# New column group bounds, an earlier residual add, an earlier mean and split last rows in a windowed-attention and feed-forward kernel on eight cores

## What is computed

```python
q = (x @ Wq + bq)  # 16 heads of 64
k = (x @ Wk + bk)  # 2 key heads
v = (x @ Wv + bv)
# each position attends to the 256 positions from 128 before to 127 after it
probs = softmax(scores);  out = probs @ v_win
x = layernorm(x + out @ Wo + bo)
# feed-forward part, x_prev is x shifted by one position
xr = mu_r * x + (1 - mu_r) * x_prev
xk = mu_k * x + (1 - mu_k) * x_prev
x = layernorm(x + sigmoid(xr @ W_r) * (square(relu(xk @ W_k)) @ W_v))
```

## Time and profile before

| | us |
|---|---|
| three runs, median (lowest to highest) | 502.43 (499.56 to 543.57) |
| the profiled execution | 499.95 |
| its span on the slowest core, core 6 | 498.4 |
| spans of the eight cores | 490.4 to 498.4 |
| PE (matmul) busy on core 6 | 424.5, 85% of the span |
| ACT, DVE, POOL busy | 331.9, 316.1, 115.7 |

### The profile page before, as it was taken

The page is one execution under the profiler, slowest core; times in us unless marked ns, Lnnn a source line. Parts: engine busy times, 40 slices in busy tenths (PEclk is TensorE's granted clock), DMA queues, the critical chain, the costliest instruction groups (busy, mean ns, idle before and its releaser), DMA issues.

```text
span 498.4 us, 10425 instructions; the slowest of 8 cores (490.4 to 498.4 us)
## 1 busy us (share of the span) xinstructions
PE 424.5 (85%) x2976; PEld 221.0 (44%) x3018; DVE 316.1 (63%) x792; ACT 331.9 (67%) x847; POOL 115.7 (23%) x297
## 2 busy tenths in 40 slices
PE   0878999689989888699799889998979989999990
PEld 0344444344444445464355345454335345464640
DVE  0046775355565667847887797997796897536321
ACT  1276879548585947685669579859669769455632
POOL 4222124022141214010123032132114033130303
PEclk9996999979989995989999999999999999999995
DMA  7999937948473758332157759766956849512112
GB/s 103 163 167 210 149 45 124 181 77 160 74 117 65 142 94 153 59 85 45 42 52 150 172 103 169 172 109 156 160 125 139 164 91 171 122 42 64 43 44 85
DMA packets 73864, 57.16 MB, mean 115 GB/s; under 512 B 59344, under 2 KB 60496, under 8 KB 73808
## 3 DMA queue, kind: packets, MB, share of 16 engines
q0 software_dynamic: 11600, 24.88, 31.9%
q1 hardware_dynamic: 62208, 31.61, 28.7%
HBM read 49.76 MB, written 8.39 MB: 117 GB/s over the span
## 4 chain that ended last, share of the span: by engine, by line
PE 55%; ACT 15%; issue 9%; DVE 9%; DMA 7%; POOL 2%; ACTq 0%; DVEq 0%; POOLq 0%; SPq 0%
PE pm L300 11%; PE pm L288 9%; PE pm L318 7%; PE pm L328 7%; PE po L353 6%; PE pm L310 5%; ACT p L392 5%; PE psc L243 4%; DVE nmax L537 4%; PE pm L267 3%; DMA zx<-xres 3%; DMA bufq<-wq 3%; ACT junk L473 2%; DVE zb L587 1%; ACT junk L490 1%
## 5 line engine op out<-in xcount | busy, mean ns | idle before, releaser
L392 ACT ACTIVATE p<-psc,nmax 128x320 bf16<-128x320 f32 x264 | 138.4, 538 | 93.8 <-DVE nmax L537 93.6
L537 DVE TENSOR_REDUCE nmax<-psc 128x2 f32<-128x640 f32 x132 | 108.0, 820 | 84.4 <-PE psc L249 84.0
L300 PE MATMUL pm<-w16o,ao 128*128 128x512 bf16 x262 | 65.9, 393 | 9.5 <-DVE zx L573 5.3
L549 DVE TENSOR_SCALAR p<-p,rall 128x320 bf16<-128x320 bf16 x264 | 62.6, 300 | 7.5 <-DVE rall L542 0.5
L288 PE MATMUL pm<-bufx,bufq 128*128 128x512 bf16 (+2 forms) x310 | 64.3, 353 | 2.6 <-issue 1.4
L310 PE MATMUL pm<-bufx,w16kf 128*128 128x256 bf16 x512 | 62.0, 277 | 2.7 <-ACT pt L406 1.6
L318 PE MATMUL pm<-w16r,bufx 128*128 128x512 bf16 x246 | 57.5, 379 | 3.9 <-ACT pt L406 1.6
L328 PE MATMUL pm<-w16vf,bufq 128*128 128x512 bf16 x247 | 58.1, 379 | 2.9 <-ACT pt L406 2.0
L392 ACT ACTIVATION_READ_ACCUMULATOR p<-psc,nmax 128x1 f32 x264 | 56.5, 214 | 0.0
L310 PEld LDWEIGHTS pm<-bufx,w16kf 128*128 128x128 bf16 x512 | 49.1, 99 | 14.1 <-issue 6.5
L243 PE MATMUL psc<-k,qy 64*128 64x320 bf16 x264 | 41.8, 314 | 11.9 <-ACT p L392 11.6
(11 more groups left out here) (75 smaller groups left out, 545.1 us busy)
## 6 DMA issues: line engine op xcount, KB each, us to landing
zx<-bo SPq DMA_DIRECT2D x17, 512.0 KB, 5.5
zx<-xres POOLq DMA_DIRECT2D x17, 512.0 KB, 6.0
out<-zb SPq DMA_DIRECT2D x16, 512.0 KB, 3.0
bufx<-xt POOLq DMA_DIRECT2D x16, 256.0 KB, 8.4
bufq<-wq POOLq DMA_DIRECT2D x4, 512.0 KB, 10.3
w16o<-wo POOLq DMA_DIRECT2D x8, 256.0 KB, 12.5
w16kf<-wkf POOLq DMA_DIRECT2D x8, 256.0 KB, 5.7
w16r<-wr POOLq DMA_DIRECT2D x8, 256.0 KB, 5.9
```

Source lines behind the costliest of these rows:

```text
L300: mm = e.matmul(pm[:, bank, :], ao[:, a % 2, kc, :], w16o[:, kc, 512 * b:512 * b + 512], start=(kc == 0), stop=(kc == KC - 1))
L392: a = e.activation(p16[:, b % 2, j // 2, g, j % 2, :], psc[:, 2 * (n % 2) + g, 0:320], AF.Exp, bias=nmax[:, n % 4, g:g + 1], accum_out=sal ...
L537: e.tensor_reduce(nmax[:, n % 4, :], psc[:, 2 * (n % 2):2 * (n % 2) + 2, 0:320], mybir.AxisListType.X, ALU.max, negate=True).then_inc(s_mx, 1)
L549: t = e.tensor_scalar(part, part, rall[:, b % 2, r:r + 1], None, ALU.mult)
```

## The change

The groups become 384, 512, 512, 512 and 448 columns wide, with explicit starts `XO`. The units of group 1 start in slot 4 and those of group 2 in slot 22; groups 3 and 4 keep their slots. `add_xres` comes four slots after `rows_y`, not six. `layer_norm` on POOL is split in two: `mean`, which waits only for the row sums, and `scale`, which waits for the squares; together they have one small instruction less. For the last 128 rows, the second sum, the squares, the final scaling and the store are done in halves of 512 columns; the second half of the final scaling goes to DVE. The core of the diff (the last rows on ACT, and the changed indexing on the host, are left out):

```diff
-XW = (512, 512, 512, 512, 320)
+XW = (384, 512, 512, 512, 448)
+XO = (0, 384, 896, 1408, 1920)
 QLO = (128, 0, 0, 0, 0)
-QHI = (512, 512, 512, 512, 192)
-GSLOT = (None, 8, 24, 36, 48)
+QHI = (384, 512, 512, 512, 320)
+GSLOT = (None, 4, 22, 36, 48)
...
-            if b % 8 == 6 or b == 0:
-                e.wait_ge(s_ea, ACT_COUNT[INDEX[("q", (b + 2) // 8, 2 * j + 1)]])
+            if b == 0 or 64 * b + 128 in XO:
+                e.wait_ge(s_ea, ACT_COUNT[INDEX[("q", group(64 * b + 128), 2 * j + 1)]])
...
+        def second_sum_half(half):
+
+            r = 2 * NH - 1
+            e.wait_ge(s_ed, DVE_COUNT[INDEX[("v", r, half)]])
+            if half == 0:
+                e.wait_ge(s_ln2, r - 1)
+            z = zb[:, r % 2, 512 * half:512 * half + 512]
+            e.scalar_tensor_tensor(z, z, 0.5, qy[:, r + 1, 4 * half:4 * half + 4, :].rearrange("p a b -> p (a b)"),
+                                   ALU.mult, ALU.add,
+                                   accum_out=st2[:, r % 2, half:half + 1]).then_inc(s_z2, 1)
...
+        r = 2 * NH - 1
+        e.wait_ge(s_ln2, r + 1)
+        e.tensor_scalar(zb[:, r % 2, 512:1024], zb[:, r % 2, 512:1024], st2[:, r % 2, 8:9], st2[:, r % 2, 9:10],
+                        ALU.mult, ALU.add).then_inc(s_oh, 1)
...
-            small(e.tensor_tensor(stat[:, 5:6], stat[:, 4:5], stat[:, 4:5], ALU.mult))
-            small(e.tensor_scalar(stat[:, 6:7], stat[:, 2:3], 1.0 / D, 1e-5, ALU.mult, ALU.add))
-            small(e.tensor_tensor(stat[:, 7:8], stat[:, 6:7], stat[:, 5:6], ALU.subtract))
+            small(e.tensor_scalar(stat[:, 5:6], stat[:, 4:5], stat[:, 4:5], 1e-5, ALU.mult, ALU.subtract))
+
+        def scale(stat, two, masked, done):
+
+            total = stat[:, 2:3]
+            if two:
+                small(e.tensor_tensor(stat[:, 6:7], stat[:, 2:3], stat[:, 11:12], ALU.add))
+                total = stat[:, 6:7]
+            small(e.tensor_scalar(stat[:, 7:8], total, 1.0 / D, stat[:, 5:6], ALU.mult, ALU.subtract))
...
+                e.wait_ge(s_ed, DVE_COUNT[INDEX[("o", tau, 1)]])
+                mean(st1[:, tau % 2, :], True)
                 e.wait_ge(s_sq1, tau + 1)
-                layer_norm(st1[:, tau % 2, :], True, tau == 0, s_ln1)
-            if n - 6 in YOUT[:NT - 2]:
-                add_xres(YOUT.index(n - 6) + 2)
+                scale(st1[:, tau % 2, :], False, tau == 0, s_ln1)
+            if n - 4 in YOUT[:NT - 2]:
+                add_xres(YOUT.index(n - 4) + 2)
```

More of the change, by code:

```diff
@@ L49, in plan_units @@
         us = [("K", g, 0), ("V", g, 0), ("W", g, 0), ("W", g, 1)] + [("q", g, dc) for dc in range(8)]
-        todo.update({n: [u] for n, u in zip(free, us)})
+        for n, u in zip(free, us):
+            todo.setdefault(n, []).append(u)
     ffn = [("k", j) for j in range(4)] + [(a, t, nh) for a in "rv" for t in range(2) for nh in range(2)]
@@ L225, in build_nc, with group @@
     s_p, s_ln1, s_ln2 = sem("s_p"), sem("s_ln1"), sem("s_ln2")
+    def group(column):
+        return max(g for g in range(5) if XO[g] <= column)
     def key_group(b):
-        return min((64 * b + 319) // 512, 4)
+        return group(64 * b + 319)
     def value_group(b):
-        return min((b // 2 + 2 + b % 2) // 4, 4)
+        return group(min(128 * (b // 2 + 2 + b % 2), XC - 1))
     def tensor(e):
@@ L411, in evac @@
                 if kind == "K":
-                    dst = k16[:, 512 * a:512 * a + XW[a]]
+                    dst = k16[:, XO[a]:XO[a] + XW[a]]
                 else:
-                    dst = vt[:, 64 + 512 * a:64 + 512 * a + XW[a]]
+                    dst = vt[:, 64 + XO[a]:64 + XO[a] + XW[a]]
                 bias = bk_s if kind == "K" else bv_s
@@ L622, in vector @@
             for u in SLOT[n - 1]:
-                if UNITS[u][0] == "v" and UNITS[u][2] == 1:
-                    second_sum(UNITS[u][1])
+                kind, r, half = UNITS[u]
+                if kind == "v" and r == 2 * NH - 1:
+                    second_sum_half(half)
+                elif kind == "v" and half == 1:
+                    second_sum(r)
             h, c = divmod(n - F0 + 10, FP)
@@ L682, in gpsimd, with mean @@
         n_p = 0
-        def layer_norm(stat, two, masked, done):
+        def mean(stat, two):
             total = stat[:, 0:1]
@@ L735, in gpsimd @@
                 r = SQ2.index(n - 1)
-                e.wait_ge(s_sq2, r + 1)
-                layer_norm(st2[:, r % 2, :], False, False, s_ln2)
+                last = r == 2 * NH - 1
+                e.wait_ge(s_z2, r + 1 + last)
+                mean(st2[:, r % 2, :], last)
+                e.wait_ge(s_sq2, r + 1 + last)
+                scale(st2[:, r % 2, :], last, False, s_ln2)
     def sync(e):
```

39 lines of the change are left out of this document (27 added, 12 removed).

## The result

The changed kernel takes 497.13 us in the median of 20 runs (493.06 to 538.92), the kernel before 501.54 (497.77 to 543.57, 20 runs). The ratio is **0.990, with a 95% interval of 0.987 to 0.993**: 5.1 us less, between 3.7 and 6.4. Of the changed kernel's 21 executions on record this ratio leaves out, besides two in which a die ran at a lower clock (such executions are left out of every comparison here), five of 500.55 to 506.99 us in which none did but one to three single cores came late, so it flatters the change a little (the plain medians differ by 4.4 us). The profiled execution took 496.12 us, where I had forecast 494.

The account below looks back on a forecast made before the run. PE was taken as the bound, losing time when idle or at its lower clock. The terms summed to -6.1 us on core 6 (span 492.3) and -2.2 on core 0 (492.6), giving 494 us, range 487 to 501.

Parts of the forecast that it names:

- the class with most of the chance: The outcome that the time stays within 2% of the kernel before, given a chance of 0.68.
- A: Lead-in: smaller group 0 brings transfers 0.6 us earlier and shortens two q units and V by 1.3; sum -1.8 us.
- B1: Slots 4 to 7: units of group 1 fill PE's waits, -1.3 us; slow clock taken as 0, bounds 0 to 3.5.
- B2: Slots 20 and 21: q units leave, PE falls short of work, +1.0 us of new idle time.
- B3: Step 19: scores wait for ACT's evacuation of the last q of group 1, which stands behind the squares; +1.8 us.
- B4: Residual of tau 2: lands 4 to 6 us earlier, 0.7 us wait left; -4.3 us core 6, -1.7 core 0.
- Below 2 us on all cores: Sign to look for: the stall before the second o unit of tau 2 shrinks to below 2 us on all cores.
- B5: Slots 4 to 47: even chance that new idle stretches drop PE's clock once more, about 2 us; taken as +1.0.
- C: Group 4: 448 columns for 320 add 4.3 us on PE, partly absorbed by idle time and clock; net +0.8 us.
- D: End: halves of the last rows shorten sum, squares and scaling, an extra store costs about 0.5; net -1.5 us.
- The shorter chain on POOL elsewhere: POOL's layer-norm chain away from the last rows: its shortening was counted as worth nothing.
- Rival (ii): Tau 2 residual lands no sooner against its need because of contention; 498.5 us, no change; chance 0.25.

Follow-up runs that it names:

- e5: Changed kernel with the residual load of tau 3 moved later and the first y-row transposes meant for slot 30, going out behind the tau 2 residual: ratio 0.985.
- e7: Changed kernel with the same transfer edits as e5 and the old column groups (512, 512, 512, 512, 320): ratio 0.988 against the kernel before.
- e6: As e5, and in slot 17 ACT evacuates q(1,7) ahead of the squares of the first rows: ratio 0.984 against the kernel before.
- e2: Changed kernel with the old column groups, all else of the change kept: ratio 0.987 against the kernel before.
- e3: Changed kernel with the residual's load put back from four to six slots behind the store of its row: ratio 0.989 against the kernel before.
- e1: Kernel before with the new column groups and their start slots alone: ratio 1.001.
- e9: Kernel before with only the mean of both layer norms worked out beside the squares: ratio 0.990.
- e8: Kernel before with only the mean beside the squares and the last rows in halves: ratio 0.992.

## Why the prediction was right, and where it was not

The predicted 494 us is close to the 496.12 of the profiled execution, the range holds both it and the median, and the class with most of the chance, within 2%, came out. The sum came out with several of its terms wrong in ways that cancelled.

**A, the lead-in.** Forecast -1.8; slot 0's exponentials start 1.8 us sooner, 24.5 to 22.7. The transfer alone gave 0.8 us on the median core (K starts at 13.83 before, at 13.06 now), where I had 0.6. The rule in the Trainium skill's page "DMA: Bandwidth & Descriptors", section "Specifications", that 512 bytes are enough for line rate, would have put K 1.7 us sooner. With e5 and e7, which differ in the groups alone, it is 1.2 us (12.95 and 14.20). So the runs lie between the rule and the price that I took from the queue's packets. From 3 to 13.5 us the queue of core 3 moved 1.36 MB in 1307 packets, where it had moved 1.40 MB in 741: shorter runs took almost nothing off its rate.

**B1, slots 4 to 7**, forecast -1.3 with K and V at full speed, bounds 0 to 3.5 for the clock. It was more. From step 4 to step 17 e5 takes 34.3 us (33.8 to 68.1) and e7, with the old groups, 30.9 (36.0 to 66.9): 3.4 us more for the 6.9 us of four more q units, so that 3.5 us of waits and of slow clock are gone. The waits in these slots were 1.3 of it; the term had the clock's share at 0, and the clock came back sooner on every core (above).

**B2, slots 20 and 21**, forecast +1.0 as new idle time, was more too. From step 19 to step 40, where the four q units are missing again, e5 takes 58.3 us and e7 62.4: 4.1 less for 6.9 less work, so +2.8. Added up from the start to step 40, new groups against old (e5 and e7, 133.3 and 134.5) win 1.2 us; A, B1, B2, B3 and B5 had said +0.7.

**B3, the new wait**, forecast +1.8, is 2.0 on every core, for the reason given: in e6, with the evacuation first, it is 0.96.

**B4, the residual**, forecast -4.3 on core 6 and -1.7 on core 0, with 0.7 us left. On seven cores nothing is left, on core 3 5.12 are. "Below 2 us on all cores" was wrong, and the bound of 5.0 was the measured value on the core that sets the time. How it went was not as described. The issue was not at 83.5 but at 84.1 to 90.6, since everything behind step 4 was later; on the middle core the landing moved from 97.2 to 95.8, not by 4 to 6 us; and PE's need did not come 4 us earlier but 2.8 later, at 98.6 for 95.8. Part of the stall was thus covered by time lost before it. With the old groups the working fits better: in e2 the landing is at 92.5, 4.7 us sooner, and no core waits over 0.2 us. That the earlier issue carries the gain of the changed kernel is not shown: e3 lacks it and is as fast.

**B5, the clock**, forecast +1.0. In most places it went the other way. The stretches at half clock in slots 4 to 8 and in group 4 became shorter or vanished (from 188 to 192 us seven cores were below 1 before, none is now). There is a small new one just behind the wait of step 19 on cores 4, 6 and 7. Core 6:

```profile
76.00:80.00 4.00, 4.00 (x20) 1.77 (x19) 1.89 (x6) 1.80 (x6) 0.76 (x2) 0.68 0.62 81
```

**C, group 4**, forecast +0.8. From step 40 to the end e5 takes 354.9 us and e7 353.4: +1.5, a difference of two single executions whose cores spread by 1 to 4 us in the part up to step 62. PE waits 1.28 and 1.77 us for ACT in the changed kernel, so the absorbed part was a little smaller than I had it.

**All terms of the groups together** were -1.8 - 1.3 + 1.0 + 1.8 + 1.0 + 0.8 = +1.5 us, a cost. e1 measured +0.6 (-1.0 to +2.1), and the changed kernel against e2 +1.5. This is the part that I had right as a sum, with B1 and B2 off in both directions.

**D, the end**, forecast 11.5 us from the last matmul, measured 11.5. How it is made up was wrong: I gave the halves about all of it, and they are 0.3 of 1.5.

**The step that failed** is the last sentence of D: "The shorter chain on POOL elsewhere is worth nothing that I count", because behind POOL's waits there was "only POOL's own later work". That work is the issue of other transfers, and they lie in the queues beside the residual. e9 puts the mean alone at -4.9 us (3.0 to 6.8), 1.2 of them in the tail. Of the rest 2.6 are seen in steps 27 to 34 of its profile, around the residual, and less in e8's. The 6 us that I gave to the earlier residual on core 6 belong to two edits: e8 and e9, with the mean and without the earlier issue, still wait up to 3.0 us, and only with both is the wait gone (e2, e7). That 494 was close to the measured time is in part luck: a gain of some 3 us that I had put at nothing stood against a core that came late by 6 us. Rival (ii), "contention makes it, not the place of the issue", was half right: contention makes the 15 us landing, but the place of the issue counts as well. Its time (498.5) was too high.

## What to carry to other kernels

An engine that issues transfers is on the path through them: three small instructions taken out of POOL's wait chain moved two transfers by 1.2 us, and that edit alone gave as much (0.990) as the whole diff. Before crediting an edit that brings a late transfer forward, ask what else shares the queues in that stretch and which of the edits moves that. Look at all cores, because the time is that of the one with the worst landing: in the profiled execution the median core gained 5.6 us and a single 15 us transfer set the result. And look in the trace whether an edit moved what it was meant to move: two of the transfers that e5 was to move stayed in their stretch.
